# Field products of 512 samples: TensorE's program as a loop over eight groups of 64, fields split 104 and 96, x loaded in GpSimd's queue

## The chip, the cores and the metric

The kernel runs on one core of one Trainium2 chip. The metric is the time of one execution on the device in microseconds (us). The median of three runs before the change is 349.12 us (348.49 to 352.26).

## What is computed

For every sample b of 512, every field i of 200 is a vector of 64 numbers, and every field has a 64 by 64 weight of its own. The fields are first multiplied by their weights, and then every mixed field is multiplied with every field of the same sample. All is in float32.

```python
# feature: (512, 200, 64)   weight: (200, 64, 64)
bilinear = jnp.einsum('bie,ied->bid', feature, weight)
out = jnp.einsum('bid,bjd->bij', bilinear, feature)   # (512, 200, 200)
```

The input is 26.2 MB of x and 3.3 MB of weights, the output 81.9 MB.

## The kernel before

Samples are handled in 4 groups of 128. Each group is split into two halves of 64 samples, and half h lives in partitions 64h to 64h+63 (`half_rows`), where the 64 partitions are the contracted numbers of a field. The weights `w_sb` stand twice in memory, once for each half. x is held as `x_sb` in three buffers of 100 fields each: two take turns for the first 100 fields of a group (`load_part0`), the third holds the last 100 (`load_part1`).

TensorE does two kinds of work, and cuts both into units that write a pair of PSUM banks each (there are four pairs, `BANK_PAIRS`):

- a **mix** multiplies 16 fields of a group by their weights. The weight of the field is the stationary operand (64 by 64), the field of 64 samples moves through it. 32 matmuls, line 210. ScalarE and VectorE copy the result into `mixed`, one bank each (lines 291 and 293).
- a **score** unit multiplies mixed fields with fields for 4 samples. The stationary operand is 64 mixed fields of one sample, a 64 by 64 block, and the 200 fields of x move through it. 8 matmuls, line 238. The 200 fields make 3 chunks of 64; the 8 fields that are left over are mixed by `tail_mix` (line 222) and scored by `tail` (line 255), 64 matmuls a unit with 32 stationary columns each.

Each operand sits in half of the array's rows and half of its columns, so four matmuls can be under way side by side, one in each quarter of the array (in the tails eight). Every matmul of float32 data in the program is two weight loads and two passes in the trace: 3648 matmuls are the 7296 passes of the page.

`walk` sets one order of units for all engines: the scores of chunk c stand among the mixes of chunk c+1. Before a unit TensorE waits until the copies of the unit four places earlier are done (`wait_banks`). The score and tail results are copied out of PSUM by ScalarE (even) and VectorE (odd), line 270, into one of 6 slots of `tile`, each of 800 KB with its two copies. The program of TensorE is written out in full: 14592 weight loads and passes.

SyncE issues every transfer. A full slot goes out to HBM (line 154), and behind some of the slots one load of x for the next group is issued: 4 loads of 800 KB (line 128) and 8 of 400 KB (line 132) for a group. A copy into a slot waits until the slot's last transfer has landed (`slot_out`). GpSimd only clears `tails` at the start (line 168).

## Time and profile before

| | |
|---|---|
| median of 3 runs | 349.12 us (348.49 to 352.26) |
| profiled execution | 347.19 us, of which 345.4 us are the span from the first to the last instruction |
| mean granted TensorE clock | 0.93 |
| TensorE passes / weight loads busy | 250.5 us (73%) / 221.2 us (64%) |
| VectorE / ScalarE / GpSimd busy | 148.4 / 128.3 / 2.4 us |
| moved by DMA | 115.70 MB, mean 335 GB/s |

Busy time of an engine is the union of its instructions' times. The ends of TensorE's passes are modelled and passes overlap, so the pace of TensorE is read from the distance between starts: the length of a run of passes by their number. "issue" in the chain and among the waits is time in which the engine had nothing to wait for that the profile shows, and yet did not run. The queue "instruction" carries the program's own instructions to the engines.

### The profile page before, as it was taken

Reading aid. Unit: us, or ns where it says so; the run is one execution under the profiler, and the core shown is the slowest. Engines: PE = TensorE matmul, PEld = TensorE weight load, DVE = VectorE, ACT = ScalarE, POOL = GpSimd, SP = SyncE. Lnnn points to the kernel's source line nnn. Section 1 sums busy time; section 2 is a strip of 40 time slices with the busy share of each in tenths; the row PEclk is TensorE's granted clock in tenths of the full one; section 3 lists DMA queues with packets and bytes.
Section 4 is the critical chain, followed back from the end, with each engine's and each line's share of the span. In section 5 each row is a group of like instructions: output and inputs, shape, how many; then the busy total and the mean of one; then the engine's idle time right before and its main releaser. Section 6 shows DMA issues by size and latency. Waiting matters only on the chain.

```text
span 345.4 us, 15674 instructions
## 1 busy us (share of the span) xinstructions
PE 250.5 (73%) x7296; PEld 221.2 (64%) x7296; DVE 148.4 (43%) x172; ACT 128.3 (37%) x177; POOL 2.4 (1%) x5
## 2 busy tenths in 40 slices
PE   0167679599967674969785967869985877987870
PEld 0156668378867573748775957748875766766760
DVE  0042455136634541605563553504653554635550
ACT  1032426045524422314452443403553444442540
POOL 2000000000000000000000000000000000000000
PEclk9987899899989988989998798989999999999995
DMA  7999998847999997757799999964899997746796
GB/s 302 423 426 423 400 368 280 331 193 289 351 409 399 395 388 261 236 242 291 300 374 418 395 366 421 306 286 194 335 373 390 407 386 312 289 199 260 284 408 286
DMA packets 21808, 115.70 MB, mean 335 GB/s; under 512 B 2416, under 2 KB 2416, under 8 KB 21360
## 3 DMA queue, kind: packets, MB, share of 16 engines
q1 hardware_dynamic: 21744, 114.70, 84.6%
q8 instruction: 58, 0.95, 1.1%
q14 instruction: 6, 0.05, 0.0%
HBM read 32.77 MB, written 81.92 MB: 332 GB/s over the span
## 4 chain that ended last, share of the span: by engine, by line
PE 72%; issue 19%; DMA 4%; DVE 1%; SPq 1%; ACT 1%
PE psum L238 46%; PE psum L210 16%; PE psum L255 9%; DMA w_sb<-w_dram 4%; PE psum L222 1%; DVE tile L270 1%; SPq L128 1%; ACT mixed L291 1%
## 5 line engine op out<-in xcount | busy, mean ns | idle before, releaser
L238 PE MATMUL psum<-x_sb,mixed 64*64 64x200 f32 x3072 | 173.2, 357 | 32.9 <-issue 29.5
L238 PEld LDWEIGHTS psum<-x_sb,mixed 64*64 64x64 f32 x3072 | 141.4, 143 | 49.5 <-issue 41.2
L270 DVE COPY tile<-psum 128x800 f32<-128x800 f32 x100 | 99.2, 992 | 141.2 <-PE psum L238 128.9
L270 ACT COPY tile<-psum 128x800 f32<-128x800 f32 x100 | 82.7, 827 | 117.2 <-PE psum L238 85.5
L210 PE MATMUL psum<-x_sb,w_sb 64*64 64x64 f32 x3072 | 67.7, 228 | 37.3 <-issue 21.3
L210 PEld LDWEIGHTS psum<-x_sb,w_sb 64*64 64x64 f32 x3072 | 65.6, 140 | 40.6 <-issue 39.5
L291 DVE COPY mixed<-psum 64x512 f32<-64x512 f32 x48 | 33.1, 689 | 28.2 <-PE psum L210 26.9
L291 ACT COPY mixed<-psum 64x512 f32<-64x512 f32 x48 | 27.9, 581 | 43.6 <-PE psum L210 43.0
L255 PE MATMUL psum<-x_sb,tails 64*32 64x200 f32 x1024 | 32.6, 377 | 13.0 <-issue 13.0
L255 PEld LDWEIGHTS psum<-x_sb,tails 64*32 64x32 f32 x1024 | 22.6, 115 | 21.7 <-issue 18.3
L293 ACT COPY mixed<-psum 128x512 f32<-128x512 f32 x24 | 14.1, 587 | 44.3 <-PE psum L210 44.2
L293 DVE COPY mixed<-psum 128x512 f32<-128x512 f32 x24 | 16.6, 692 | 17.6 <-PE psum L210 17.6
L222 PE MATMUL psum<-x_sb,w_sb 64*64 64x64 f32 x128 | 4.6, 220 | 0.5
L222 PEld LDWEIGHTS psum<-x_sb,w_sb 64*64 64x64 f32 x128 | 4.2, 132 | 0.9 <-issue 0.9
L300 ACT COPY tails<-psum 128x512 f32<-128x512 f32 x4 | 2.3, 586 | 0.3
L168 POOL MEMSET tails<- 128x2560 f32 x1 | 2.2, 2232 | 0.3 <-POOLq L324 0.3
L293 ACT ACT_TABLE_LOAD x1 | 1.3, 1283 | 0.7 <-PEq L324 0.7
L324 POOL MEMSET const-bfloat16-1.0<- 128x1 bf16 x1 | 0.1, 103 | 0.0
L324 POOL MEMSET const-uint8-127<- 128x1 uint8 x1 | 0.1, 102 | 0.0
L324 POOL MEMSET const-float32-0.0<- 128x1 f32 x1 | 0.1, 100 | 0.2 <-issue 0.2
L324 POOL MEMSET const-float32-1.0<- 128x1 f32 x1 | 0.1, 100 | 0.0
## 6 DMA issues: line engine op xcount, KB each, us to landing
out_dram<-tile SPq DMA_DIRECT2D x96, 800.0 KB, 6.3
x_sb<-x_dram SPq DMA_DIRECT2D x16, 800.0 KB, 8.7
x_sb<-x_dram SPq DMA_DIRECT2D x32, 400.0 KB, 7.7
w_sb<-w_dram SPq DMA_DIRECT2D x2, 2048.0 KB, 16.7
out_tail_dram<-tile SPq DMA_DIRECT2D x4, 800.0 KB, 4.5
w_sb<-w_dram SPq DMA_DIRECT2D x1, 2304.0 KB, 22.5
```

The lines of the kernel that those rows point to most:

```text
L128: eng.dma_start(x_sb[:, 2 * (g % 2), quads], x[g, 0, :, quads]).then_inc(part0_loaded[g % 2], 16)
L168: nc.gpsimd.memset(tails[:], 0.0).then_inc(zeroed, 1)
L210: last = nc.tensor.matmul(psum[half_rows(h ^ swap), bank + swap, r * HALF_SAMPLES:(r + 1) * HALF_SAMPLES], w_sb[half_rows(h), field, :], x ...
L222: last = nc.tensor.matmul(psum[half_rows(h), n % BANK_PAIRS * 2, r * HALF_SAMPLES:(r + 1) * HALF_SAMPLES], w_sb[half_rows(h), TAIL_FIRST + ...
L238: last = nc.tensor.matmul(psum[half_rows(pair), n % BANK_PAIRS * 2 + h, a * FIELDS:(a + 1) * FIELDS], mixed[half_rows(h), (CHUNKS * g + c) ...
L255: last = nc.tensor.matmul(psum[tile4 * TAIL_TILE:(tile4 + 1) * TAIL_TILE, n % BANK_PAIRS * 2 + h, piece * FIELDS:(piece + 1) * FIELDS], we ...
L270: copy(tile[:, k % SLOTS, engine], psum[:, bank:bank + 2, 0:2 * FIELDS]).then_inc(copied[engine], 1)
L291: copy(to[half_rows(h)], source[half_rows(1 - h)]).then_inc(copied[engine], 1)
L293: copy(to, source).then_inc(copied[engine], 1)
L300: copy(tails[:, :, :, 0:TAIL], source).then_inc(copied[engine], 1)
L324: nc = bacc.Bacc("TRN2", target_bir_lowering=False, num_devices=1)
```

## The change

The groups are now 8, of 64 samples each, and a sample's 200 fields are split over the two halves of the partitions: fields 0 to 103 in the lower one, 104 to 199 in the upper one. One copy of the weights is enough. The tails are gone.

- A **score** unit has 2 samples. Now x is the stationary operand, in blocks of 104 and 96 columns (`x_now`), and the 200 mixed fields of the sample move through it (`mixed`). That is 4 matmuls of 104 or 96 by 200 in place of 8 of 64 by 200 for 4 samples. Two of them can be under way side by side, one in each half of the array's rows. There are 32 score units in a group.
- A **mix** is as before in shape (64 by 64, 64 samples moving). There are 8 mix units in a group, of 32, 16 and 8 matmuls (`MIX`), 200 matmuls together. They come after the score units named in `MIX_AFTER`, and only ScalarE copies them, into `made`.
- The moving operand must hold all 200 fields in both halves of the partitions, and the stationary one must stand at addresses that are the same in every group. So VectorE copies `made` into `mixed` in 8 steps a group of three copies each (`place`), and GpSimd copies x from `x_in` into `x_now`, also in 8 steps, with samples and fields exchanged. Both have one buffer.
- TensorE's program is the mixes of group 0, then a loop (`Fori`) of 7 rounds whose body is one group's 32 scores with the 8 mixes of the next group, then the last group's scores. The body has 328 matmuls. Semaphore values in it are read from registers that are worked out in each round.
- x of the next group (3.3 MB, four transfers issued together) is loaded in GpSimd's queue, when GpSimd has placed the last step of the current one. Out go 614 KB and 26 KB for 4 samples, from one of 4 slots in place of 6.
- ScalarE copies 20 of 32 score units (`engine_of`), VectorE 12.

```diff
-GROUPS = 4
-HALVES = 2
-QUADS = BATCH // GROUPS // 4
-HALF_SAMPLES = 2 * QUADS
...
+GROUPS, SLOTS = 8, 64
+MAIN, REST = 96, 8
+TOP = MAIN + REST
+PIECES = 3
+PIECE = MAIN // PIECES
+MIX = [(16 * m, 8, 2) for m in range(5)] + [(80, 4, 2), (88, 4, 2), (MAIN, 4, 1)]
+MIXES = len(MIX)
+MADE = FIELDS // 2
...
+UNIT_SAMPLES = 2
+SCORES = SLOTS // UNIT_SAMPLES
+MIX_AFTER = (7, 9, 12, 14, 17, 20, 22, 24)
+UNITS = SCORES + MIXES
+STEPS = 8
+STEP_SLOTS = SLOTS // STEPS
+STEP_UNITS = STEP_SLOTS // UNIT_SAMPLES
+NEXT_STEPS_AFTER = {28: 0, 30: 1}
+STEPS_AFTER = {STEP_UNITS * n + 2: n + 2 for n in range(STEPS - 2)}
+EXPANSIONS = 3
+TILE_UNITS = 2
+TILES = SCORES // TILE_UNITS
+TILE_SLOTS = 4
...
+def engine_of(u):
+    return 0 if u % 2 == 0 or u % 8 == 7 else 1
...
+def order(g):
+    for u in range(SCORES):
+        yield "score", g, u
+        if u in MIX_AFTER and g + 1 < GROUPS:
+            yield "mix", g + 1, MIX_AFTER.index(u)
...
+    w_sb = sb("w_sb", [128, TOP, EMB])
+    x_in = sb("x_in", [128, TOP, SLOTS])
+    x_now = sb("x_now", [128, SLOTS, TOP])
+    made = sb("made", [128, 2, SLOTS, MADE])
+    mixed = sb("mixed", [128, SLOTS, FIELDS])
+    tile = sb("tile", [128, TILE_SLOTS, 2, TILE_UNITS, UNIT_SAMPLES * FIELDS])
...
+            for g in range(GROUPS):
+                for t in range(TILES):
+                    k = g * TILES + t
+                    s = k % TILE_SLOTS
+                    for u in range(TILE_UNITS * t, TILE_UNITS * (t + 1)):
+                        e = engine_of(u)
+                        sp.wait_ge(copied[e], COPIES[NUMBER["score", g, u]][e])
+                    sp.dma_start(out[g, t], tile[0:MAIN, s]).then_inc(slot_out[s], 16)
+                    sp.dma_start(out_rest[g, t], tile[MAIN:TOP, s, 0]).then_inc(slot_out[s], 16)
...
         @block.gpsimd
         def _(pool):
+            for p in range(PIECES + 1):
+                load_x(pool, 0, p)
+            nc.gpsimd.memset(x_in[half_rows(1), MAIN:TOP, :], 0.0).then_inc(zeroed, 1)
+            pool.wait_ge(zeroed, 1)
+            for g in range(GROUPS):
+                for p in range(PIECES + 1):
+                    pool.wait_ge(x_loaded[p], 16 * (g + 1))
+                for c in range(STEPS):
+                    if g > 0:
+                        pool.wait_ge(unit_ready, NUMBER["score", g - 1, (c + 1) * STEP_UNITS - 1] + 1)
+                    slots = slice(c * STEP_SLOTS, (c + 1) * STEP_SLOTS)
+                    nc.gpsimd.tensor_copy(
+                        x_now[:, slots, :], x_in[:, :, slots].rearrange("p f s -> p s f")).then_inc(x_placed, 1)
+                if g + 1 < GROUPS:
+                    pool.wait_ge(x_placed, STEPS * (g + 1))
+                    pool.wait_ge(unit_ready, NUMBER["mix", g, MIXES - 1] + 1)
+                    for p in range(PIECES + 1):
+                        load_x(pool, g + 1, p)
...
+            def score(n, u):
+                bank = n % BANK_PAIRS * 2
+                for a in range(UNIT_SAMPLES):
+                    slot = UNIT_SAMPLES * u + a
+                    for h, rows in enumerate((TOP, MAIN)):
...
+                            psum[0:rows, bank + h, a * FIELDS:(a + 1) * FIELDS],
+                            x_now[half_rows(h), slot, 0:rows], mixed[half_rows(h), slot, :], start=True, stop=True)
...
+            def wait_step(g, u):
+                if u % STEP_UNITS == 0:
+                    steps = u // STEP_UNITS + 1
+                    pe.wait_ge(x_placed, g * STEPS + steps)
+                    pe.wait_ge(mixed_placed, g * (EXPANSIONS * STEPS) + EXPANSIONS * steps)
...
+            with pe.Fori(0, GROUPS - 1) as g:
+                x_there = 16 * g + 32
+                pe.compute_val(x_there)
+                for kind, to, k in order(1):
+                    n = NUMBER[kind, to, k]
+                    (free, value), = banks_free(n, g)
+                    pe.compute_val(value)
+                    if kind == "mix":
+                        pe.wait_ge(w_loaded[piece_of(k)], 16)
+                        pe.wait_ge(free, value)
+                        pe.wait_ge(x_loaded[piece_of(k)], x_there)
+                        mix(n, k)
+                    else:
+                        pe.wait_ge(free, value)
+                        wait_step(g, k)
+                        score(n, k)
...
+            def place(g, c):
+                if c == 0:
+                    eng.wait_ge(copied[0], COPIES[NUMBER["mix", g, MIXES - 1]][0])
+                if g > 0:
+                    eng.wait_ge(unit_ready, NUMBER["score", g - 1, (c + 1) * STEP_UNITS - 1] + 1)
+                slots = slice(c * STEP_SLOTS, (c + 1) * STEP_SLOTS)
+                copy(mixed[:, slots, 0:MADE], made[:, g % 2, slots, :]).then_inc(mixed_placed, 1)
+                for h in range(2):
+                    copy(mixed[half_rows(h), slots, MADE:FIELDS],
+                         made[half_rows(1 - h), g % 2, slots, :]).then_inc(mixed_placed, 1)
+            if engine == 0:
+                for m in range(MIXES):
+                    mix(0, m)
+            else:
+                for c in NEXT_STEPS_AFTER.values():
+                    place(0, c)
+            for g in range(GROUPS):
+                for kind, to, k in order(g):
+                    if kind == "mix":
+                        if engine == 0:
+                            mix(to, k)
+                        continue
+                    if engine_of(k) == engine:
+                        score(g, k)
+                    if engine == 1 and k in STEPS_AFTER:
+                        place(g, STEPS_AFTER[k])
+                    if engine == 1 and k in NEXT_STEPS_AFTER and g + 1 < GROUPS:
+                        place(g + 1, NEXT_STEPS_AFTER[k])
```

How the change moves instructions shows at three places. On TensorE, before, in the middle of group 0, a score unit is 8 matmuls, and a mix of 32 stands between two of them:

```order
L238 MATMUL psum<-x_sb,mixed 64x200 x7
L210 MATMUL psum<-x_sb,w_sb 64x64 [waits w_loaded1,part0_loaded0,copied_act]
L210 MATMUL psum<-x_sb,w_sb 64x64 x31
L238 MATMUL psum<-x_sb,mixed 64x200 [waits part1_loaded4,copied_dve]
L238 MATMUL psum<-x_sb,mixed 64x200 x7
```

On TensorE, after, inside the loop's body where steps of placing are awaited (`x_placed`, `mixed_placed`) and a mix of the next group follows:

```order
L219 REGISTER_ALU [waits copied_dve]
L220 REGISTER_ALU [waits x_placed]
L210 MATMUL psum<-mixed,x_now 104x200 [waits mixed_placed]
L210 MATMUL psum<-mixed,x_now 96x200
L210 MATMUL psum<-mixed,x_now 104x200
L210 MATMUL psum<-mixed,x_now 96x200
L236 REGISTER_ALU
L198 MATMUL psum<-x_in,w_sb 64x64 [waits x_loaded1,copied_act,w_loaded1]
L198 MATMUL psum<-x_in,w_sb 64x64 x31
```

A score unit went from 8 matmuls to 4, and the stationary operand alternates between 104, 96 and 64 columns. The end of the body, and what follows it:

```order
L210 MATMUL psum<-mixed,x_now 96x200
L230 REGISTER_ALU
L230 COMPARE_AND_BRANCH
L210 MATMUL psum<-mixed,x_now 104x200 [waits mixed_placed,x_placed,copied_act]
```

The branch goes back to the body's first instruction six times. On GpSimd, which had one memset, the rows of one group now are:

```order
L169 COPY x_now<-x_in 128x832 [waits x_loaded3,x_loaded2,unit_ready,x_loaded1,x_loaded0]
L169 COPY x_now<-x_in 128x832 [waits unit_ready] x7
L126 DMA x_in<-x_dram 128x2048 [waits unit_ready,x_placed]
L126 DMA x_in<-x_dram 128x2048 x2
L128 DMA x_in<-x_rest_dram 64x512
```

The loads of a group stand behind the eight copies of the group before, and the last of these waits for that group's predecessor to be scored to its end.

## Rows read from the trace of the kernel before

**Rows 1.** The page: engines, DMA queues (packets, MB, share), chain.

```profile
PE 250.5 (73%) x7296; PEld 221.2 (64%) x7296; DVE 148.4 (43%) x172; ACT 128.3 (37%) x177; POOL 2.4 (1%) x5
...
q8 instruction: 58, 0.95, 1.1%
...
PE 72%; issue 19%; DMA 4%; DVE 1%; SPq 1%; ACT 1%
```

**Rows 2.** The page's groups: busy us, mean ns of one, idle before.

```profile
L238 PE MATMUL psum<-x_sb,mixed 64*64 64x200 f32 x3072 | 173.2, 357 | 32.9 <-issue 29.5
...
L270 DVE COPY tile<-psum 128x800 f32<-128x800 f32 x100 | 99.2, 992 | 141.2 <-PE psum L238 128.9
L270 ACT COPY tile<-psum 128x800 f32<-128x800 f32 x100 | 82.7, 827 | 117.2 <-PE psum L238 85.5
...
L255 PE MATMUL psum<-x_sb,tails 64*32 64x200 f32 x1024 | 32.6, 377 | 13.0 <-issue 13.0
...
L168 POOL MEMSET tails<- 128x2560 f32 x1 | 2.2, 2232 | 0.3 <-POOLq L324 0.3
```

**Rows 3.** The chain that ended last, 107 to 124 us: start, us, what.

```profile
108.07 1.80 issue
...
113.95 1.99 issue
...
119.98 3.40 issue
123.37 3.32 PE psum L238 x40
```

**Rows 4.** The same chain near 80 us, where fewer transfers were under way.

```profile
77.17 1.82 PE psum L238 x30
...
81.52 0.61 issue
```

**Rows 5.** Windows: us, busy by engine, clock, DMA share, GB/s.

```profile
2.80:15.90 13.10, 0.00 (x0) 0.00 (x0) 0.00 (x0) 0.00 (x0) 0.16 (x1) 1.00 1.01 423
15.90:21.30 5.40, 5.31 (x221) 5.33 (x222) 2.35 (x4) 2.03 (x4) 0.00 (x0) 1.00 1.03 414
77.60:79.20 1.60, 1.60 (x46) 1.53 (x46) 0.62 (x1) 0.66 (x1) 0.00 (x0) 1.00 0.17 58
116.00:121.00 5.00, 3.98 (x126) 3.56 (x126) 2.63 (x3) 2.81 (x4) 0.00 (x0) 1.00 1.00 379
325.00:333.00 8.00, 8.00 (x186) 7.86 (x182) 5.33 (x7) 4.96 (x6) 0.00 (x0) 1.00 1.02 411
334.00:345.40 11.40, 0.28 (x8) 0.00 (x0) 0.99 (x1) 0.45 (x1) 0.00 (x0) 0.66 0.77 314
```

**Rows 6.** TensorE's timeline near 70 and 155 us: start, us, run of passes.

```profile
70.77 1.13 PE L210 MATMUL psum<-x_sb,w_sb 64*64 64x64 f32 x64
71.71 1.62 PE L238 MATMUL psum<-x_sb,mixed 64*64 64x200 f32 x32
...
155.38 1.61 PE L238 MATMUL psum<-x_sb,mixed 64*64 64x200 f32 x32
156.92 3.09 PE L255 MATMUL psum<-x_sb,tails 64*32 64x200 f32 x128
159.94 0.41 PE L238 MATMUL psum<-x_sb,mixed 64*64 64x200 f32 x4
```

**Rows 7.** TensorE's timeline at the end, 321 to 334 us.

```profile
321.13 13.15 PE L238 MATMUL psum<-x_sb,mixed 64*64 64x200 f32 x288 [1.96 <-ACT mixed L291]
```

**Rows 8.** Weight loads of lines 238 and 210 alone: ns min/median/max.

```profile
L238 PEld LDWEIGHTS psum<-x_sb,mixed x284: 132/133/138, 321.1 to 333.6; 64*64 64x64 f32 x142
...
L210 PEld LDWEIGHTS psum<-x_sb,w_sb x66: 129/132/136, 78.6 to 81.3; 64*64 64x64 f32 x66
L210 PE MATMUL psum<-x_sb,w_sb x65: 215/217/269, 78.8 to 81.3; 64*64 64x64 f32 x65
```

**Rows 9.** DMA queues between 21.3 and 23.9 us.

```profile
q8 instruction: 1, 0.02, 2.7%
```

More of the change, by code:

```diff
@@ L102, with position @@
-COPIES, NUMBER, OUT_TILES = count_copies()
-TILE_OF = {tile: k for k, tile in enumerate(OUT_TILES)}
-def build(nc, x, weight, out, out_tail):
-    sb = lambda name, shape: nc.alloc_sbuf_tensor(name, shape, F32)
-    w_sb = sb("w_sb", [128, FIELDS, EMB])
-    x_sb = sb("x_sb", [128, 3, QUADS, PART, 2])
-    mixed = sb("mixed", [128, 2, QUADS, CHUNK, 2])
-    tails = sb("tails", [128, HALF_SAMPLES // 4, 4, TAIL_TILE + TAIL])
-    tile = sb("tile", [128, SLOTS, 2, HALVES, 2 * FIELDS])
+def position(m):
+    return sum(width * banks for _, width, banks in MIX[:m])
@@ new lines, in engine_of, with fields_by_position @@
+def engine_of(u):
+    return 0 if u % 2 == 0 or u % 8 == 7 else 1
+def fields_by_position():
+    made = [[], []]
+    for first, width, banks in MIX:
+        if first == MAIN:
+            for h in range(2):
+                made[h] += range(first + h * width, first + (h + 1) * width)
+        else:
+            for bank in range(banks):
+                for h in range(2):
+                    a = h * TOP + first + bank * width
+                    made[h ^ bank] += range(a, a + width)
+    return [made[h] + made[1 - h] for h in range(2)]
@@ new lines, in order @@
+def order(g):
[3 more added lines that the diff above has]
+            yield "mix", g + 1, MIX_AFTER.index(u)
+def count_copies():
+    copies, number = [], {}
+    units = [("mix", 0, m) for m in range(MIXES)] + [unit for g in range(GROUPS) for unit in order(g)]
+    a = d = 0
+    for n, (kind, g, k) in enumerate(units):
+        engine = 0 if kind == "mix" else engine_of(k)
+        a, d = a + (engine == 0), d + (engine == 1)
+        copies.append((a, d))
+        number[kind, g, k] = n
+    return copies, number
@@ new lines, with build @@
+COPIES, NUMBER = count_copies()
+STRIDE = [COPIES[MIXES - 1 + UNITS][e] - COPIES[MIXES - 1][e] for e in range(2)]
+def build(nc, x, x_rest, weight, weight_rest, out, out_rest):
+    sb = lambda name, shape: nc.alloc_sbuf_tensor(name, shape, F32)
+    w_sb = sb("w_sb", [128, TOP, EMB])
[4 more added lines that the diff above has]
+    tile = sb("tile", [128, TILE_SLOTS, 2, TILE_UNITS, UNIT_SAMPLES * FIELDS])
@@ L166, in _ @@
+            for s in range(TILE_SLOTS):
+                sp.wait_ge(slot_out[s], 32 * (GROUPS * TILES // TILE_SLOTS))
         @block.gpsimd
         def _(pool):
-            nc.gpsimd.memset(tails[:], 0.0).then_inc(zeroed, 1)
+            for p in range(PIECES + 1):
[14 more added lines that the diff above has]
+                    pool.wait_ge(unit_ready, NUMBER["mix", g, MIXES - 1] + 1)
+                    for p in range(PIECES + 1):
+                        load_x(pool, g + 1, p)
@@ L226, in tail_mix @@
                 last.then_inc(unit_ready, 1)
-            def score(n, g, c, t, u):
-                wait_banks(n)
-                if t == 0 and u == 0:
-                    wait_copies(NUMBER["mix", g, c, MIX_UNITS - 1])
-                if c == 0 and u == 0:
-                    wait_part1(g, t)
-                for a in range(2):
-                    quad = 4 * t + 2 * u + a
-                    for pair in range(2):
-                        for h in range(HALVES):
-                            last = nc.tensor.matmul(
-                                psum[half_rows(pair), n % BANK_PAIRS * 2 + h, a * FIELDS:(a + 1) * FIELDS],
-                                mixed[half_rows(h), (CHUNKS * g + c) % 2, quad, :, pair],
-                                x_sample(g, h, quad, pair), start=True, stop=True)
-                last.then_inc(unit_ready, 1)
@@ new lines, in wait_step @@
+            def wait_step(g, u):
[4 more added lines that the diff above has]
+            for m in range(MIXES):
+                n = NUMBER["mix", 0, m]
+                for free, value in banks_free(n):
+                    pe.wait_ge(free, value)
+                pe.wait_ge(x_loaded[piece_of(m)], 16)
+                pe.wait_ge(w_loaded[piece_of(m)], 16)
+                mix(n, m)
@@ L335 @@
[L335 to L342 removed]
+    r = run_bass_kernel_spmd(nc, [inputs], core_ids=[0]).results[0]
```

274 lines of the change are left out of this document (79 added, 195 removed).

## Prediction

> **What bounds the kernel now.** I read the page first. The queue that carries instructions brought 0.95 MB in 58 packets, 16 KB each, for 14592 weight loads and passes of TensorE, which is 64 bytes an instruction and 256 in a packet; "issue" is 19% of the chain, 66 us [rows 1]. Then the chain itself: its issue pieces end at 109.87, 115.94 and 123.38 us [rows 3]. Between the last two ends lie 7.4 us, and about 128 passes with their 128 loads, so one packet. The reader is to see that TensorE runs through a packet in about 4 us and then waits for the next. DMA engines are full in such a stretch (share 1.00 at 116 to 121) and nearly empty (0.17) near 78 us, where a block ran from about 77.2 and the wait behind it ended at 82.1 after 0.61 us of idling, 4.9 us for a block [rows 4, 5]. So a packet takes some 5 to 7.4 us from the start of the block before it, and longer the more data is ahead of it. The store holds little: from 15.9 to 21.3 us 443 instructions ran and none was fetched, and the first fetch shows right behind them [rows 5, 9]. With what ran before them that is about two packets' worth.
>
> DMA itself is the second limit: it reaches 411 to 423 GB/s [rows 5]. VectorE and ScalarE are below half [rows 1].
>
> The pace of TensorE without waits: scores, 288 passes start within 12.8 us (13.15 less the 0.36 of one pass), 44.5 ns a pass, or 178 ns for four side by side [rows 2, 7]. Mixes, 64 passes in 0.94 us, 14.7 ns a pass. Tails, 128 in 3.02 us, 23.6 ns [rows 6]. Over the kernel: 3072 x 44.5 = 137, 3200 x 14.7 = 47, 1024 x 23.6 = 24, together 208 us. With 16 us ahead and 11.4 us behind that is 235 of 345; the waits for instructions are 66, the lower clock some 17 (below), and about 27 are spread over the small gaps between units.
>
> **The change, part by part.** I sum the span of the changed kernel.
>
> *Scores.* A pass still has 200 moving columns, so 178 ns, but only two fit side by side, 89 ns a pass. 8 groups x 32 units x 4 matmuls x 2 passes = 2048 passes, 182 us; 22.8 us a group. Scores and tails were 161 us, so this alone costs 21 us. Each pass needs 104 or 96 new stationary columns. The load of 64 columns shows 133 ns, beside passes that are repeated every 178 [rows 7, 8]. By columns alone 104 take at most 133 x 104/64 = 216 ns, at least 133. I take them as hidden: in a mix the 64-column loads are repeated every 59 ns although each shows 132 [rows 6, 8], so the most of it is not the array's time. The high end is a rival.
>
> *Mixes.* The same 3200 passes at 14.7 ns, 5.9 us a group.
>
> *Switches.* Scores now use half of the array's rows and 104 columns, mixes quarters. Before, only scores and tails differed: 32 score passes ahead of a tail took 1.54 us where 32 x 44.5 is 1.42, and the 128 tail passes end 0.12 later than at the pace of 178 ns for eight [rows 6]. No row has a mix on one side. Its bounds are 0 and the 0.22 us that a mix's pass shows [rows 8], on top of the 0.12. I take 0.14 into a mix and 0.25 out of it, 0.39 for a mix, 3.1 us a group. From zero to 0.6 for a mix it is 0 to 4.8 a group.
>
> *Start.* Weights and x of group 0 are 6.55 MB, 15.5 us at 423 GB/s from 2.8 us on, so 18.3 us. Now no score can start before all of it is mixed, copied and placed: one short mix, its copy and three copies of VectorE, 3 us more, first score at 21.3. Before it started at 26.6, with a twelfth of the mixes done in place of an eighth.
>
> *Copies.* VectorE has 12 score copies of 992 ns a group [rows 2] and 24 placing copies of 800 numbers. The nearest row is the same 992 ns for 800 numbers out of PSUM, the low end half of it. 24 to 36 us a group, under the period of 43 that comes out below, so hidden on average. ScalarE: 20 x 0.83 and some 7 us of mixes, 24 us. If VectorE is at the high end, the four steps placed around a group's end make it late by 1 or 2 us there.
>
> *GpSimd.* A step copies 832 numbers per partition, strided. The only row writes 2560 in 2.23 us, 0.73 us for 832 [rows 2]. A copy that reads as well, with strides, may take several times that; I take 2. Loading x takes about 14 us from the group's end on, then eight steps: 30 us, hidden below 43. The cover is gone at 3.6 us a step.
>
> *Outputs and DMA.* A group is 10.5 MB out and 3.3 in, 33 us at 420 GB/s, again below 43. In the last group nothing but scores is left, and there the outputs set the pace, 10.5 MB at 411 to 423 GB/s, 25 us. SyncE's second transfer for a slot lies beside these. Behind the last score came 11.4 us with six slots filled [rows 5]; with four, smaller ones I take 7.
>
> Without waits for instructions: 21.3 + 7 x (22.8 + 5.9 + 3.1) + 25 + 7 = 276 us.
>
> *Instructions.* A body of 328 matmuls is 1312 instructions and some 75 for registers, 5.4 packets. By the 443 that ran before the first fetch, it can't stay in the store, and is fetched again in each round. What changes is the pace of use. Scores alone take 16 instructions per 0.71 us, 11.4 us a packet: hidden. Between the first and the last mix, 17 score units and 8 mixes hold some 1150 instructions in 21 us, 4.7 us a packet, against 5 to 7.4 for the next to come. Three terms:
> - The branch back, six times. Its target isn't the next packet, so its wait starts when TensorE is at the end: 5 to 7.4 us, less what stands in TensorE's own queue. The end of a group is full of outputs, which speaks for 7. I take 4.5, from 2.5 to 7: 27 us (15 to 42).
> - The packet fetched behind the x load. 3.3 MB are issued at once, 8 us of DMA, when the group begins; outputs and instructions queue behind them. A fetch near 11 us into the group finds 6 us of data ahead. 3 us a group (1 to 5), 21 us (7 to 35). The wait for slots that get free late falls in the same stretch and costs nothing more.
> - The rest of the mixing stretch: DMA is at two thirds there, the next packet comes in about 5. 1.2 us a group (0 to 3), 8 us (0 to 21).
>
> *Clock.* While it is granted half, 40 passes take 3.32 us, 83 ns a pass in place of 44.5 [rows 3]. Its mean was 0.93 with 66 us of such waits, and it fell behind the longer ones, which I put at 17 us. With 56 us of waits I take 12 (4 to 17). *Small gaps:* 27 over 232 changes between kinds of unit; the switches take part of them already. 7.
>
> The Trainium skill ("TensorE: Matmul & The Clock Gate", LDWEIGHTS) gives a load's time as its columns over 1.2 GHz, an estimate of 87 ns for 104 columns. By it the loads are hidden, as in the sum.
>
> 276 + 27 + 21 + 8 + 12 + 7 = 351 us of span, and 1.8 around it, 353 us, against 347.2 of the profiled execution, whose own median is 349.1. Beside the kernel before, the waits, the clock and the gaps give back 35 us (110 to 75) and the end 4; two side by side in place of four cost 21, the switches 22, the outputs of the last group 2.
>
> **Rivals.** *Short queues* (faster): with fewer transfers in flight a packet comes in 4 to 5 us everywhere, as near 78 us. Branch 2.5 x 6 = 15, x load 7, no more in the mixing stretch, clock 5, gaps 7: 276 + 34 + 1.8 = 312. For it: 0.17 of DMA share in a stretch [rows 5], and four slots that limit the backlog. Against: outputs of a score-only stretch ask for 450 GB/s, more than DMA gives.
>
> *The body stays in the store.* Then no fetch in the loop: 276 + 4 + 7 + 1.8 = 289, just above the floor that DMA sets, 111.4 MB at 420 GB/s, 265 us. Against it stand the 443 instructions. The Trainium skill ("Runtime: NRT & Kernel Launch", Instruction fetch mechanics) says both: 128 KB for TensorE, in which 1387 instructions would fit, and a window of two blocks of 16 KB that works as a FIFO, out of which a taken branch stalls. The rows stand for the second.
>
> *Long queues* (slower): every fetch finds full queues. 42 + 35 + 14 + 17 + 7 = 115: 393. It decides from about 6 us a branch.
>
> *GpSimd sets the pace:* loading and eight steps must fit in a group, 14 + 8 steps against 43 us, so it decides from 3.6 us a step. At 4 us a group takes 46 in place of 43: 21 us more, 374; at 5 us 430. For it: the strides, of which no row tells; against it, 3.6 us are five times the memset's pace.
>
> *Loads exposed:* at the high end of 216 ns a pair of passes waits 38 ns, 1024 pairs, 39 us: 392.
>
> **How the numbers follow.** Forecast, 335 to 372: 0.45. Short queues, 305 to 335: 0.27. Body stays: 0.05. Long queues, 372 to 400: 0.13. GpSimd 0.06, loads 0.04. The range 311 to 388 leaves out about 2 in 10. About 1% is what a measurement of this kernel tells from no change, 345.6 to 352.6; of the forecast's 0.45 I give 0.12 to below it, 0.13 to it, 0.20 above. So faster 0.44, same 0.13, slower 0.43. The time is that of the forecast.
>
> **What would show it.** The issue waits come once at each branch, 3 to 6 us, six times, some 44 us apart, and once about 11 us into a group; the instruction queue brings 40 to 50 packets (few, if the body stays). Score passes repeat every 178 ns in pairs. A step of GpSimd is 1 to 3 us. The mean DMA rate is near 320 GB/s. The prediction is wrong if the branch costs under 2 us, if pairs take over 200 ns, or if TensorE waits for `x_placed`.

## The result, and the profile after

The changed kernel takes 379.89 us in the median of four runs (376.64 to 382.13), the kernel before 348.81 (347.68 to 352.26) on the same chip: a ratio of 1.087 (1.074 to 1.099). It is 9% slower. The forecast of 353 us is 27 us short of it, inside the stated range, and only 4 us above the kernel before; faster had 0.44 and slower 0.43, so the direction was hardly forecast at all. Its waits add up to about what was measured, but their cause is another. Runs of one kernel spread by up to some 4%; times below are medians of all runs, and the ratios leave out runs that are over 1.5% above the fastest of their kernel. The profiled execution took 377.92 us, of which 376.1 are the span.

The page of the changed kernel: engines, DMA queues (packets, MB, share), chain.

```profile
PE 281.6 (75%) x5248; PEld 238.1 (63%) x5248; DVE 235.8 (63%) x288; ACT 177.4 (47%) x225; POOL 134.8 (36%) x101
...
q8 instruction: 10, 0.16, 0.2%
...
DMA 35%; PE 28%; DVE 16%; issue 8%; POOL 4%; SPq 3%; ACT 3%; ACTq 0%; DVEq 0%; POOLq 0%
DMA out_rest_dram<-tile 27%; PE psum L210 20%; PE psum L198 8%; DVE mixed L289 7%; DVE tile L265 5%; DMA x_in<-x_rest_dram 5%; POOL x_now L169 4%; DMA x_in<-x_dram 4%; DVE mixed L287 3%; SPq L150 3%; ACT tile L265 3%; SPq L151 0%; POOL x_in L126 0%; ACTq L130 0%; ACTq L263 0%
...
L265 ACT COPY tile<-psum 104x800 f32<-104x800 f32 x160 | 129.6, 830 | 158.9 <-DMA out_rest_dram<-tile 91.7
L169 POOL COPY x_now<-x_in 128x832 f32<-128x832 f32 x64 | 114.8, 1817 | 198.9 <-DMA x_in<-x_rest_dram 105.1
...
L289 DVE COPY mixed<-made 64x800 f32<-64x800 f32 x128 | 100.2, 782 | 4.0
...
x_in<-x_dram POOLq DMA_DIRECT2D x24, 1024.0 KB, 12.0
```

Ten packets of instructions stand where there were 58 [rows 1], and "issue" is 8% of the chain in place of 19%. The change did what it says. But the chain is now led by DMA, 35%: 27% is the wait of a copy for a slot of `tile` whose last transfer has not landed, the rest are loads of x. VectorE comes third with 16%, where it had 1%.

The waits of the changed kernel: engine, line, released by, us in total, times, longest.

```profile
POOL x_now L169 <- DMA x_in<-x_rest_dram: 105.1, 7, 19.1
...
ACT tile L265 <- DMA out_rest_dram<-tile: 91.7, 45, 7.4
...
DVE tile L265 <- DMA out_rest_dram<-tile: 44.0, 15, 9.5
...
PE psum L198 <- DMA x_in<-x_dram: 26.7, 7, 11.1
...
PE psum L198 <- issue: 20.6, 8, 4.0
```

Of the 20.6 us of "issue" 3.8 lie in the start and 5.5 within two mixes of the loop's first round, where the body is fetched for the first time. Another 10.9 stand before the first mix of three later groups. There the mix starts 0.1 us behind ScalarE's copy of the fourth unit before it, which had itself waited for a slot (ScalarE, then TensorE):

```profile
88.64 0.83 ACT L265 COPY tile<-psum 104x800 f32<-104x800 f32 x1 [6.54 <-DMA out_rest_dram<-tile]
...
89.56 1.73 PE L198 MATMUL psum<-x_in,w_sb 64*64 64x64 f32 x64 [3.97 <-issue]
```

So these are waits for slots and x, not for instructions.

One such wait shows whole at 250 us. The timeline of GpSimd, then the chain, then VectorE's timeline (start, us, what):

```profile
245.69 1.65 POOL L169 COPY x_now<-x_in 128x832 f32<-128x832 f32 x1 [1.83 <-PE psum L210]
248.39 1.60 POOL L169 COPY x_now<-x_in 128x832 f32<-128x832 f32 x1 [1.06 <-PE psum L210]
250.29 1.76 POOL L126 DMA_DIRECT2D x_in<-x_dram  x3 [0.30 <-POOL x_now L169]
```

```profile
247.80 0.57 DVE mixed L289
248.40 2.02 DVE mixed L289
...
252.84 0.04 issue
252.88 12.49 DMA out_rest_dram<-tile
```

```profile
246.57 1.20 DVE L287 COPY mixed<-made 128x800 f32<-128x800 f32 x1
247.80 2.63 DVE L289 COPY mixed<-made 64x800 f32<-64x800 f32 x2
...
261.00 0.99 DVE L265 COPY tile<-psum 104x800 f32<-104x800 f32 x1 [3.77 <-DMA out_rest_dram<-tile]
```

GpSimd has placed its last step and issues 3.3 MB of x at once, at 250.29. A small output issued right behind, at 252.88, lands 12.49 us later. VectorE has no slot until 261.00. TensorE goes on until its banks are full. The same rows show a second thing: the copy at 248.40 takes 2.02 us, its twin a moment before 0.57. GpSimd's own copy runs from 248.39 to 249.99; behind its end 0.43 us are left of the 2.02.

Windows (us, busy by engine, clock, DMA share, GB/s), with x in flight, without it, over the middle of the kernel, and in the last group:

```profile
217.00:227.00 10.00, 8.65 (x184) 7.18 (x188) 2.60 (x4) 4.21 (x5) 0.00 (x0) 0.70 1.02 423
195.00:205.00 10.00, 8.60 (x128) 7.54 (x128) 7.42 (x11) 4.79 (x7) 3.52 (x3) 1.00 0.78 238
40.00:340.00 300.00, 243.81 (x4578) 206.35 (x4576) 202.09 (x249) 151.85 (x194) 115.53 (x80) 0.90 0.90 310
335.00:365.00 30.00, 24.44 (x248) 19.51 (x250) 24.05 (x34) 14.46 (x18) 1.92 (x1) 1.00 0.95 306
```

At first x moves nearly alone and slowly. It was issued from 207.12 us on. Between 211 and 213 us its queue (q0) moves 0.37 MB, that of the outputs (q1), with a transfer of 614 KB issued at 210.51, 0.01 MB:

```profile
q0 software_dynamic: 45, 0.37, 75.0%
q1 hardware_dynamic: 7, 0.01, 1.7%
```

In the last group nothing but outputs moves, DMA's share is 0.95, and yet it is 306 GB/s, where the same situation gave 411 before [rows 5].

TensorE's timeline, at the start and at the last group:

```profile
20.49 1.61 PE L198 MATMUL psum<-x_in,w_sb 64*64 64x64 f32 x92 [0.34 <-DMA x_in<-x_dram]
24.22 1.54 PE L198 MATMUL psum<-x_in,w_sb 64*64 64x64 f32 x52 [2.12 <-issue]
31.25 7.03 PE L210 MATMUL psum<-mixed,x_now 64*104 64x200 f32 x56 [5.49 <-DVE mixed L289]
...
329.80 4.98 PE L210 MATMUL psum<-mixed,x_now 64*104 64x200 f32 x56
335.58 5.66 PE L210 MATMUL psum<-mixed,x_now 64*104 64x200 f32 x56 [0.80 <-DVE mixed L289]
...
364.31 1.60 PE L210 MATMUL psum<-mixed,x_now 64*104 64x200 f32 x16 [0.33 <-ACT tile L265]
```

So the span is 31.3 us to the first score, seven groups of 43.5 (304.3), the last group 30.3, and 10.2 behind it. The forecast's sum was 21.3, seven of 42.5, 25 and 7.

### The profile page after: what moved, and what is told of

The parts are those of the page before. It is cut to its first block, busy times and chain, and to the rows that moved or that the text cites. A ratio compares the mean times of both kernels' runs of the same rounds, so it can differ in the third digit from the quotient of the medians.

```text
span 376.1 us, 12288 instructions
## 1 busy us (share of the span) xinstructions
PE 281.6 (75%) x5248; PEld 238.1 (63%) x5248; DVE 235.8 (63%) x288; ACT 177.4 (47%) x225; POOL 134.8 (36%) x101
## 4 chain that ended last, share of the span: by engine, by line
DMA 35%; PE 28%; DVE 16%; issue 8%; POOL 4%; SPq 3%; ACT 3%; ACTq 0%; DVEq 0%; POOLq 0%
DMA out_rest_dram<-tile 27%; PE psum L210 20%; PE psum L198 8%; DVE mixed L289 7%; DVE tile L265 5%; DMA x_in<-x_rest_dram 5%; POOL x_now L169 4%; DMA x_in<-x_dram 4%; DVE mixed L287 3%; SPq L150 3%; ACT tile L265 3%; SPq L151 0%; POOL x_in L126 0%; ACTq L130 0%; ACTq L263 0%
## 5 line engine op out<-in xcount | busy, mean ns | idle before, releaser
L210 PE MATMUL psum<-mixed,x_now 64*96 64x200 f32 (+1 forms) x2048 | 216.7, 359 | 37.0 <-DVE mixed L289 14.9
L210 PEld LDWEIGHTS psum<-mixed,x_now 64*96 64x96 f32 (+1 forms) x2048 | 175.1, 175 | 63.5 <-DVE tile L265 20.4
L265 ACT COPY tile<-psum 104x800 f32<-104x800 f32 x160 | 129.6, 830 | 158.9 <-DMA out_rest_dram<-tile 91.7
L169 POOL COPY x_now<-x_in 128x832 f32<-128x832 f32 x64 | 114.8, 1817 | 198.9 <-DMA x_in<-x_rest_dram 105.1
L265 DVE COPY tile<-psum 104x800 f32<-104x800 f32 x96 | 94.4, 991 | 100.5 <-PE psum L210 54.3
L198 PE MATMUL psum<-x_in,w_sb 64*64 64x64 f32 x3200 | 71.9, 241 | 47.3 <-DMA x_in<-x_dram 26.7
L198 PEld LDWEIGHTS psum<-x_in,w_sb 64*64 64x64 f32 x3200 | 63.0, 152 | 64.0 <-issue 51.4
L289 DVE COPY mixed<-made 64x800 f32<-64x800 f32 x128 | 100.2, 782 | 4.0
L277 ACT COPY made<-psum 128x1024 f32<-128x1024 f32 (+1 forms) x64 | 53.2, 832 | 32.1 <-PE psum L198 31.9
L287 DVE COPY mixed<-made 128x800 f32<-128x800 f32 x64 | 46.4, 725 | 26.2 <-ACT made L277 26.2
```

What stands on the lines that cost most here:

```text
L169: nc.gpsimd.tensor_copy(x_now[:, slots, :], x_in[:, :, slots].rearrange("p f s -> p s f")).then_inc(x_placed, 1)
L198: last = nc.tensor.matmul(psum[half_rows(h ^ swap), bank + (swap if banks == 2 else 0), r * SLOTS:(r + 1) * SLOTS], w_sb[half_rows(h), fie ...
L210: last = nc.tensor.matmul(psum[0:rows, bank + h, a * FIELDS:(a + 1) * FIELDS], x_now[half_rows(h), slot, 0:rows], mixed[half_rows(h), slot ...
L265: copy(tile[0:TOP, k % TILE_SLOTS, :, u % TILE_UNITS, :], psum[0:TOP, bank:bank + 2, 0:UNIT_SAMPLES * FIELDS]).then_inc(copied[engine], 1)
L277: copy(made[:, g % 2, :, at:at + width * banks].rearrange("p s (k r) -> p s k r", k=banks), psum[:, bank:bank + banks, 0:width * SLOTS].re ...
L287: copy(mixed[:, slots, 0:MADE], made[:, g % 2, slots, :]).then_inc(mixed_placed, 1)
```

## The experiments

All were timed beside the kernel before; its median was 347.2 us beside e1 to e4, 350.5 beside e5 to e8 and 347.4 beside e9 to e12.

**e1_unrolled: the loop alone undone.** TensorE's seven groups are written out, all else stays.

```diff
-            with pe.Fori(0, GROUPS - 1) as g:
-                x_there = 16 * g + 32
...
-                for kind, to, k in order(1):
+            for g in range(GROUPS - 1):
+                for kind, to, k in order(g):
```

> TensorE's program is written out in full again, 10496 weight loads and passes; nothing else differs. The changed kernel fetched 10 packets of instructions in all and waits little for them. Theory A (its time goes into outputs and x that queue for DMA, with four slots): written out it needs about 42 packets and some of them come late in the mixing stretches, but part of that falls into waits that are there anyway: 376 us of span becomes 380 to 395. Theory B (the branch back costs 4 to 5 us, six times, as I predicted): without it 350 to 365.

383.5 us (374.3 to 388.7) against 379.9, in theory A's 380 to 395. The packets are back:

```profile
q8 instruction: 41, 0.67, 0.7%
```

31 packets more, and no difference that four runs can tell. In this kernel fetched instructions cost next to nothing, and so the loop saves next to nothing.

**e2_no_x: x is loaded for group 0 only**, and groups 1 to 7 compute with it; the waits of TensorE and GpSimd are for the first load.

```diff
-                    for p in range(PIECES + 1):
-                        load_x(pool, g + 1, p)
```

> The loads of x for groups 1 to 7 are left out, so the results of these groups are those of group 0's x; all placing and all matmuls stay. Theory A: the 5 us wait of TensorE for x at the first mix of each group and the waits for slots in the same stretch go, 7 groups by 6 to 8 us, span 320 to 335. Theory C (VectorE's placing, with GpSimd on the same memory port, sets the pace): 360 to 372. Theory D (two matmuls side by side and the switches set the pace): above 365.

326.8 us (324.9 to 328.8), 0.941 of before (0.929 to 0.952), in theory A's 320 to 335. Loading x costs 53 us, 7.6 a group, though its 23 MB, 54 us of DMA at 423 GB/s, were to lie beside TensorE's work. What is left is outputs alone, and DMA is full of them at a low rate (window as above):

```profile
115.00:120.00 5.00, 5.00 (x160) 4.51 (x160) 4.88 (x7) 3.65 (x5) 1.83 (x1) 1.00 0.96 294
```

**e3_x_spread: x in small pieces between the outputs.** SyncE loads x in pieces of 16 fields, one behind each of the tiles 0 to 4, 6 and 7 of a group.

```diff
-PIECES = 3
+PIECES = 6
+X_AFTER = (0, 1, 2, 3, 4, 6, 7)
...
+                    if t in X_AFTER and g + 1 < GROUPS:
...
+                        load_x(sp, g + 1, X_AFTER.index(t))
```

> x and weights are loaded in pieces of 16 fields (six in place of three, and the rest), and x is issued by SyncE, one piece behind each of the output tiles 0 to 4, 6 and 7 of a group, in place of GpSimd's queue and one burst. Theory A: the outputs no longer stand behind 3.3 MB, and the first mix waits for a sixth of x alone: span 345 to 362. Theories C and D: within 5 us of 376.

400.6 us (398.1 to 401.4), ratio 1.151: slower, and outside both expectations. x lands late, GpSimd then does its eight steps in a row, and VectorE's placing copies beside it take 1.02 us in the mean in place of 0.78:

```profile
DMA x_in<-x_dram 21%; PE psum L209 20%; DVE mixed L288 14%; PE psum L197 12%; DVE tile L264 6%; DVE mixed L286 4%; DMA out_rest_dram<-tile 4%; SPq L153 2%; ACT tile L264 2%; SPq L152 2%; SPq L138 1%; SPq L127 0%; ACTq L131 0%; ACT made L276 0%; SPq L151 0%
...
L288 DVE COPY mixed<-made 64x800 f32<-64x800 f32 x128 | 130.5, 1019 | 4.0
```

The waits for slots are gone from the chain (27% to 4%), as meant. What replaced them is x itself.

**e4_x_burst: the same burst as in the kernel after, issued by SyncE behind tile 0.**

```diff
+                    if t == 0 and g + 1 < GROUPS:
+                        sp.wait_ge(x_placed, STEPS * (g + 1))
...
+                        for p in range(PIECES + 1):
+                            load_x(sp, g + 1, p)
```

> x is issued by SyncE, all four pieces of a group at once, behind output tile 0; otherwise as the changed kernel. If the burst is what costs (theory A), outputs now stand strictly behind it and the time is 372 to 390. If it is GpSimd's queue itself (a slower kind of queue, or a late issue), the time falls to 355 to 365.

384.0 us (381.8 to 386.6), as expected if the burst is what costs (372 to 390). The queue that issues x is not the cause. The waits only trade places: ScalarE's for slots fall from 91.7 to 59.5 us, TensorE's for x rise from 26.7 to 53.0.

**e5_out_128: the same output bytes from all partitions.** Each tile's 96 x 6400 bytes leave as 128 x 4800 bytes; the rows sent are not the rows computed. GpSimd also clears half of `tile` at the start (5.4 us, while x is loading; the first score stands at 31.30 us as before).

```diff
-                    sp.dma_start(out[g, t], tile[0:MAIN, s])
+                    sp.dma_start(out[g, t]...rearrange("(q r) -> q r", q=128), tile[:, s]...[:, 0:1200])
```

> The 614 KB of a full slot go out from 128 partitions with 4800 bytes each in place of 96 partitions with 6400 bytes each; the bytes and the number of transfers stay, the output holds the wrong rows. Theory P (new, from the run without x: outputs alone fill the DMA engines at 300 to 320 GB/s, where before, from 128 partitions, they reached 411 to 424): outputs go at 400 or more, span 335 to 355. Theory A (only the burst of x and the four slots matter): outputs are not slow by themselves, so 368 to 380.

363.3 us (358.7 to 366.6), ratio 1.043 (1.028 to 1.058): 17 us less, between the two expectations. ScalarE's wait for slots falls from 91.7 to 63.9 us, VectorE's from 44.0 to 17.0. Most of this comes from the seven groups. The last group takes 29.1 us (324.61 to 353.70) in place of 30.3, and 9.2 us follow in place of 10.2. Its outputs reach a higher rate than the 306 of 96 partitions, but not the 411 of the kernel before (window, clock, DMA share and GB/s as above):

```profile
336.00:352.00 16.00, 12.97 (x128) 9.54 (x126) 11.71 (x17) 8.01 (x10) 0.00 (x0) 1.00 0.94 349
```

**e6_small_out: 6 of 96 rows of a tile are sent.**

```diff
-                    sp.dma_start(out[g, t], tile[0:MAIN, s])
+                    sp.dma_start(out[g, t, 0:6], tile[0:6, s])
```

> Of the 614 KB of a slot 38 KB go out (6 of 96 rows); all waits stay. This takes the outputs out of DMA. Theories A and P: the waits for slots and most of the wait for x go, span 295 to 315. Theory C (VectorE and GpSimd on one port): above 340. Theory D (the array's pace): above 330.

328.7 us (327.9 to 329.5), which none of the expectations had. Outputs cost 51 us. But 329 is 40 above the 289 that the forecast gave for a kernel in which nothing is late, and here slots hardly are (ScalarE waits 9.0 us for them, VectorE 1.6):

```profile
PE 40%; DVE 30%; issue 13%; DMA 12%; POOL 2%; ACT 1%; ACTq 0%; DVEq 0%; POOLq 0%
PE psum L210 29%; DVE mixed L289 15%; DMA x_in<-x_dram 12%; PE psum L198 12%; DVE tile L265 9%; DVE mixed L287 6%; POOL x_now L169 2%; ACT made L277 0%; POOL x_in L126 0%; ACTq L130 0%; ACT tile L265 0%; DVEq L263 0%; POOLq L174 0%; POOLq L333 0%
...
PE psum L210 <- DVE tile L265: 21.0, 18, 1.9
...
PE psum L210 <- DVE mixed L289: 14.0, 8, 6.0
```

The last two rows are waits. TensorE waits for VectorE's copies, 29 us behind the start (6.0 of the 35 are the start), where before the first mixes of later groups it waits 1.4 us or less. With the outputs gone VectorE is what is late.

**e7_pace: e6, and no x and no placing copies behind group 0.** TensorE does all its matmuls, all results are copied out of PSUM.

```diff
-                for c in range(STEPS):
+                for c in range(STEPS if g == 0 else 0):
...
-                    for p in range(PIECES + 1):
-                        load_x(pool, g + 1, p)
...
-                    if engine == 1 and k in STEPS_AFTER:
+                    if engine == 1 and g == 0 and k in STEPS_AFTER:
```

> As the run with small outputs, and also without the loads of x for groups 1 to 7 and without the placing copies of GpSimd and VectorE behind group 0. All matmuls, mixes, switches, score copies and the loop's branches stay: it is the price of TensorE's program alone. By my prediction's terms, start 25, scores 182, mixes 41 behind the start, switches 22, end 3, branches 6 x 4.5: 300. By the trace of the changed kernel (169 ns a pair of passes, little wait at a branch): 262 to 275.

274.8 us in one run, 274.9 in the other, in the 262 to 275 that the trace had given. TensorE is busy 91% of the span of 273.1, and the branch back costs nothing that shows: the second of the timeline's rows below crosses a branch without a gap. From the first score (31.50) to the last pass (269.33) it takes 237.8 us; the forecast's terms give 7 x 31.8 + 22.8 = 245.

```profile
PE 248.0 (91%) x5248; PEld 226.3 (83%) x5248; DVE 114.5 (42%) x120; ACT 177.1 (65%) x225; POOL 16.8 (6%) x17
...
31.50 7.69 PE L207 MATMUL psum<-mixed,x_now 64*104 64x200 f32 x56 [6.08 <-DVE mixed L281]
...
90.83 10.39 PE L207 MATMUL psum<-mixed,x_now 64*104 64x200 f32 x120
...
254.79 14.54 PE L207 MATMUL psum<-mixed,x_now 64*104 64x200 f32 x170
```

The 170 passes of the last row are 85 pairs in 14.54 less 0.36 us, 167 ns a pair. So 105 us lie between this and the kernel after. Taking x out gives 53, taking outputs out 51, and both together with the placing copies 105. The parts overlap: from e6 to e7 it is 54 us for x and the placing copies together, and no run splits these. Some 34 of the 105 us are no waits at all. The same 5248 passes keep TensorE busy for 281.6 us in the kernel after and 248.0 here, with a mean granted clock of 0.90 there and 0.98 here.

**e8_no_pool: GpSimd places x for group 0 only**; it still loads every group's x.

```diff
-                for c in range(STEPS):
+                for c in range(STEPS if g == 0 else 0):
```

> GpSimd places x for group 0 alone, and issues the loads of x at the same points; scores of later groups use group 0's x. Theory C: VectorE's placing copies, 1.17 us for two of 64 partitions when GpSimd is quiet and up to 3.8 beside it, return to 0.6 each, and the span falls by 20 or more, to under 356. Theories A and P: DMA still sets the pace, span 362 to 376.

363.1 us in the median of two (359.4, 366.8), some 17 us less (13 to 21). That is what theories A and P expected (362 to 376), not the 20 or more of theory C. VectorE's placing copies fall to the time that one takes alone:

```profile
L288 DVE COPY mixed<-made 64x800 f32<-64x800 f32 x128 | 77.0, 601 | 4.0
...
L286 DVE COPY mixed<-made 128x800 f32<-128x800 f32 x64 | 38.6, 603 | 26.4 <-ACT made L276 26.4
```

This mixes two effects: shorter copies, and a load of x that no longer waits for GpSimd's last step. A third, TensorE not waiting for `x_placed`, is none: no such wait shows in the kernel after. Slots now are the limit, ScalarE's waits for them are 102.5 us. e9 was to part the two effects.

**e9_x_by_scalar: ScalarE places x in groups 1 to 7.**

```diff
+X_STEPS_AFTER = {8: 0, 12: 1, 14: 2, 18: 3, 22: 4, 26: 5, 28: 6, 31: 7}
...
+                    if engine == 0 and k in X_STEPS_AFTER and g + 1 < GROUPS:
...
+                        copy(x_now[:, slots, :], x_in[:, :, slots]...).then_inc(x_placed, 1)
```

> The whole computation; x of groups 1 to 7 is placed into x_now by ScalarE (a step of 8 slots behind the score copies of units 8, 12, 14, 18, 22, 26, 28 and 31 of the group before), group 0 by GpSimd as ever; GpSimd goes on loading x. Theory P (copies of GpSimd and VectorE stretch each other; leaving GpSimd's steps out gave 363 against 380): VectorE's placing copies come down from 0.78 to about 0.6 us, 358 to 370 us. ScalarE's 56 further copies at 0.8 to 1.1 us are 45 to 62 us on an engine that is busy for 177 of 376 and waits 92 for slots, so hidden. Rival L (what leaving out the steps gave was that TensorE no longer waits for x_placed): with the steps as late as before, 372 to 385. Rival S: ScalarE, which also copies the mixes, becomes late in the second half of a group: over 385.

414.1 us (411.3 to 418.2), ratio 1.206, the slowest of all, and the over 385 of rival S. VectorE's copies did come down, to 0.60 us. But a step takes ScalarE 1.66 us, not 0.8 to 1.1, and the group's x reaches it late (group row; then TensorE's and ScalarE's timelines):

```profile
L313 ACT COPY x_now<-x_in 128x832 f32<-128x832 f32 x56 | 92.9, 1659 | 31.7 <-DMA x_in<-x_rest_dram 31.7
...
240.00 1.98 PE L198 MATMUL psum<-x_in,w_sb 64*64 64x64 f32 x64 [8.16 <-DMA x_in<-x_dram]
...
248.99 1.59 ACT L313 COPY x_now<-x_in 128x832 f32<-128x832 f32 x1 [4.54 <-DMA x_in<-x_rest_dram]
```

TensorE waits 8.16 us for x before the first mix, where the kernel after waits 3 to 6 in rounds 2 to 7. Then ScalarE, at unit 8, waits 4.54 us for the last small piece of x, with the mix and score copies that TensorE needs queued behind it. This is rival S, with a wait that the expectation had not seen. What it costs that copies of VectorE and GpSimd hold each other up stays open: in this kernel no run gave more for it than e8.

**e10_128_scalar: e9 with the output layout of e5**, both edits as shown there and the clearing of e5, among them

```diff
-                    sp.dma_start(out[g, t], tile[0:MAIN, s])
+                    sp.dma_start(out[g, t]...rearrange("(q r) -> q r", q=128), tile[:, s]...[:, 0:1200])
```

> e9 and the layout of outputs of e5 together: ScalarE places x, and 96 x 6400 bytes of a tile leave as 128 x 4800 bytes (the rows sent are then not the rows computed; all else is as in the kernel after). Theory: the two costs, 16 us each, lie in different stretches (outputs in the second half of a group, placing copies around its end) and add: 342 to 358 us. Rival: both are the same wait seen from two sides, since a slot freed late and a copy made late end in the same wait of TensorE for banks: 358 to 368, no better than the better of the two alone.

392.4 us (391.2 to 394.3). This is neither expectation, since e9 had failed; but it is 22 us under e9, as e5 is 17 under the kernel after. The layout of the outputs is worth 17 to 22 us in two kernels with different waits. x lands sooner too, a median of 11.8 us behind its issue in place of 14.3.

**e11_double_body: two groups in the loop's body**, three rounds, the seventh group written out.

```diff
-            with pe.Fori(0, GROUPS - 1) as g:
+            with pe.Fori(0, (GROUPS - 2) // 2) as r:
+              for half in range(2):
+                g = 2 * r + half
```

> TensorE's loop has three rounds of two groups each, some 2700 instructions in the body, and group 6 is written out. Theory B (the store holds 2048 instructions, as the Trainium skill has it in Runtime: NRT & Kernel Launch, Instruction fetch mechanics; a body of 1387 stays, one of 2700 can't): every round fetches again, 35 to 45 packets in the instruction queue against 10, and the time is that of the kernel written out, 376 to 390 us. Rival (the store, or what keeps a body, is larger): some 20 packets, each once, and 374 to 384 us. The time can hardly tell them apart, the packets do.

381.2 us (376.1 to 386.4), and 45 packets, as theory B expected (35 to 45) and not the rival (some 20):

```profile
q8 instruction: 45, 0.74, 0.7%
```

A body of some 2700 instructions is fetched in every round, one of 1387 is not. The time is that of the kernel after and of e1: the three medians are within 1%.

**e12_before_small: the kernel before with 8 of 128 rows of a tile sent.**

```diff
-                sp.dma_start(to, tile[:, k % SLOTS])
+                sp.dma_start(to[0:8], tile[0:8, k % SLOTS])
```

> The kernel before with 8 of the 128 rows of each output tile sent, all else as it was: what the waits for instructions cost when hardly any data is in the queues. Theory Q (a packet of instructions takes as long as the data ahead of it): 57 packets at the 4.9 us seen near 78 us, against blocks that run in 4 to 4.5 us, leave 0.5 to 0.9 us each, 30 to 50 us in place of 66; with the clock given back and no wait for slots 290 to 320 us. Rival R (a packet's delay is fixed, about 6 us): issue stays above 60 us and the time at 325 to 345. In the kernel after the same edit gave 328.7, so under Q the kernel before is the faster one without outputs too.

270.3 us (264.7 to 276.1), 0.776 of before (0.759 to 0.793). Faster than either expectation. It fetches the same 58 packets:

```profile
q8 instruction: 58, 0.95, 1.4%
...
PE 85%; issue 5%; DMA 5%; DVE 2%; SPq 1%; ACT 0%
```

"issue" is 5% of 265 us, 13 us, where it was 66 [rows 1]. The clock is 0.99 in place of 0.93. So some 53 of those 66 us come and go with the outputs. That is theory Q, packets standing behind data, with more to it than was expected. The time falls by 77 us, so it is not the whole: the clock and what else waited for outputs are in it too.

## Why the prediction came out in its range and was wrong in cause

**The step that failed: "it can't stay in the store".** The forecast took the 443 instructions ahead of the first fetch as the size of the store, 5.4 packets a group for the body, and three terms of 27, 21 and 8 us. The body stays: 10 packets in all. Beyond the 5.5 us of the first round none of the three terms shows, and e7, with 10 packets as well, has no gap at a branch. So the 443 instructions don't say how much is kept. That they say how far fetching runs ahead is the reading that is left; no run tests it. By the forecast's own signs it is wrong: it named a branch under 2 us as one, and looked for 40 to 50 packets. Of the other two signs neither came (pairs over 200 ns, TensorE waiting for `x_placed`). The case was among the rivals, at 0.05 and 289 us. That no packet comes in the loop came true, its time did not, since it took every other wait as small. The Trainium skill ("Runtime: NRT & Kernel Launch", Instruction fetch mechanics) gives TensorE 128 KB, 2048 instructions, and the same section a window of two blocks out of which a branch stalls. The runs agree with the first, a body of 1387 kept and one of some 2700 not (e11); they don't agree with the second, since six branches back over 1387 instructions, more than five blocks, show no stall.

**What stands in their place: three waits that the forecast priced at nothing.** Together with the slower passes behind them they are 82 us in seven groups (43.5 against 31.8 a group), near the 75 that the forecast had put on instructions, clock and gaps. That the total came out near is chance. The figures below overlap and do not add up.

- *Loading x, 53 us (e2).* The forecast let "the wait for slots that get free late" cost nothing beside a late packet. `x_in` is one buffer. It can be loaded only when GpSimd has placed its last step, which is when the next group begins, and the first mix stands 8 units in. The forecast held the 14 us of loading against GpSimd's eight steps, never against that mix, which by its own 0.71 us a unit is due after 5.7 us. In rounds 2 to 7 it starts 10.7 to 13.7 us behind the group's first score. 3.3 MB go out in one burst, for some 4 us hardly an output moves beside them, the four slots fill, and TensorE stops. The window at 217 to 227 us shows it: 423 GB/s, share 1.02, and the clock at 0.70 behind the wait. Spreading the load (e3) takes the slot waits away and makes x too late for its mixes. The cure for one is the other's ill while x has one buffer and the load starts at the group's begin. A second buffer, six slots in place of four, or a first mix that stands later were not run.
- *Outputs from 96 partitions, 17 to 22 us (e5, e10).* The forecast took 420 GB/s for outputs, from rows of a kernel that sends 128 partitions. The last group ran at 306 at a share of 0.95. The last group and the end took 8.5 us more than planned; e5 took back only some 2 of them, at 349 GB/s, so the most of that is not the layout, and stays open. The Trainium skill ("SBUF — State Buffer", Door 1: the DMA port swizzle) has partitions 0 to 63 on one half of the ports and 64 to 127 on the other. With 96 partitions the first half carries two thirds of the bytes, an estimate of 3/4 of the full rate, 308 to 317 of 411 to 423. The 306 agrees with that. No run here sent partitions in another choice, and e5 makes the rows shorter as well, so the ports themselves are argued, not shown; that the layout costs some 17 us is shown.
- *VectorE and GpSimd, some 17 us together with an earlier load of x (e8).* The forecast put a placing copy at 0.5 to 1 us and looked for trouble only in the load of each engine. It saw VectorE late by 1 or 2 us around a group's end if copies are slow, but left this out of the sum; TensorE waits there 0.7 to 2.2 us, 9.4 us in seven groups. A placing copy alone takes 0.57 us; beside a copy of GpSimd it ends behind it: the copies of 246.57 and 248.40 both end 0.43 us after GpSimd's does (247.34 and 249.99). This agrees with the exclusive lock that the Trainium skill ("SBUF — State Buffer", SBUF: two separate sides) describes for a pair of ports these two engines share. Copies out of PSUM, line 265, stay at 0.99. VectorE is 30 us busier for it (235.8 against 205.4 in e8), on the path of the placed operands.

**The start, 10 us.** First score at 31.3, not 21.3. x was waited for until 20.5, where the forecast had its loads done at 18.3, and 2.1 us more went on instructions that run here for the first time, so the last mixes end at 25.8. Then 5.5 us go on the copies in a row, beside GpSimd's, in place of the 3 for mix and copies.

**What held.** The pace of pairs was put at 178 ns and is 167. Loads of 104 columns are hidden. The array's time with switches was 245 us by the sum and is 238 (e7). A step of GpSimd was put at 2 us and takes 1.82. "Loads exposed" and "GpSimd sets the pace" are out. The clock term did not hold: it was put at 12 us, and slower passes are some 34. The clock, 0.90 in the mean, falls behind the waits for slots and x, as between 217 and 227 us (0.70).

**Why it is slower than before.** The change saves the fetching, but fetching was late in the kernel before mainly because the outputs fill DMA. With hardly any outputs the kernel before takes 270 us (e12), the kernel after 329 (e6). The written-out program by itself was not the limit. The changed kernel has nothing to set against that: even with outputs, x and placing copies gone it takes 275 us (e7), no less than the 270 of the kernel before with outputs gone alone, and the placing copies and x in a burst come on top.

## What to carry to other kernels

Time that an engine waits for instructions can be a symptom of full DMA queues: cut the bytes in an experiment, leave the program alone, and see whether the waits go, before a loop is built against them. A single buffer that is refilled between its last and its next use turns a load into a burst, and whatever shares DMA with it, output slots first, has to stand it. Ask of each output how many of the 128 partitions it leaves from, and of each pair of VectorE and GpSimd copies in SBUF whether they fall together.

## Not expected of the hardware

- TensorE keeps a loop of 1387 instructions and runs its seven rounds on one fetch, 10 packets in the whole kernel; a body of some 2700 brings 45.
- Outputs of 614 KB from 96 partitions go out at 294 to 306 GB/s with DMA at a share of 0.95; 128 partitions gave 349 at 0.94 with the same bytes (e5) and 411 in the kernel before.
- A placing copy of VectorE (800 numbers, SBUF to SBUF) takes 0.57 us alone and up to 2.02 beside a GpSimd copy.
- ScalarE's copy of 832 numbers between SBUF tensors with the two inner dimensions exchanged takes 1.66 us; its copy of 800 numbers from PSUM 0.83.
- Waits for instructions fall from 66 to 13 us when outputs shrink to a sixteenth, with the same 58 packets.
